# Cross-attention on one core: the next tile's transposes moved to the second half of a period's first block, and the first attention tile's low half moved from GpSimd to VectorE

## The reference, cut to what matters

```
def block_forward(x, codebook_embeds, codebook_mask, ...):
    xn = layer_norm(x, ln0_w, ln0_b)
    q, k, v = (heads of xn @ qkv_w.T)
    sa = merge(softmax(q @ k.T * SCALE) @ v) @ sa_proj_w.T
    x = x + sa
    xn = layer_norm(x, ln1_w, ln1_b)
    q = heads(xn @ q_w.T)
    k = heads(codebook_embeds @ k_w.T)
    v = heads(codebook_embeds @ v_w.T)
    attn = softmax(q @ k.T * SCALE + bias)
    x = x + merge(attn @ v) @ ca_proj_w.T
    xn = layer_norm(x, ln2_w, ln2_b)
    return x + (gelu(xn @ fc1_w.T + fc1_b) @ fc2_w.T + fc2_b)
```

## Time and profile before

| | |
|---|---|
| median of 3 runs | 3499.25 us (3497.89, 3499.25, 3512.89) |
| profiled execution | 3504.63 us, span 3502.8 us |
| PE busy, share of the span | 3281.3 us, 94% |
| DVE, ACT, POOL busy | 2078.2, 1541.9, 1553.9 us |
| mean granted clock of PE | 0.963 |
| cross phase in the trace | about 2058 to 2606 us |

### The profile page before, as it was taken

One profiled execution on the slowest core, in us unless ns is written; L12 is line 12 of the kernel. 1 busy time (PEld: TensorE's weight loads), 2 busy tenths in 40 slices (PEclk: granted clock), 3 DMA queues, 4 the chain that ended last, 5 costly groups with the idle time before them and its releaser, 6 DMA issues. The chain is left out here.

```text
span 3502.8 us, 44500 instructions
## 1 busy us (share of the span) xinstructions
PE 3281.3 (94%) x16812; PEld 2133.4 (61%) x16812; DVE 2078.2 (59%) x3643; ACT 1541.9 (44%) x2826; POOL 1553.9 (44%) x495
## 2 busy tenths in 40 slices
PE   7998999999999999999999959898969599999999
PEld 5885555555555555555555346656537488888887
DVE  4444887777778777777877136767657532222222
ACT  2321566666666666666666513443434321111111
POOL 0001578878887887888788723343401000000000
PEclk9997899999999999999999979999989899999999
DMA  4446265565557556555653554433337621111110
GB/s 169 179 169 182 56 149 117 113 155 129 121 126 152 123 109 150 124 125 126 151 119 83 106 150 137 125 113 119 101 125 274 242 103 41 41 45 48 41 44 25
DMA packets 195909, 420.93 MB, mean 120 GB/s; under 512 B 33601, under 2 KB 56711, under 8 KB 176239
## 3 DMA queue, kind: packets, MB, share of 16 engines
q1 hardware_dynamic: 172399, 281.75, 26.0%
q0 software_dynamic: 18432, 134.23, 19.0%
q10 hardware_dynamic: 4864, 2.11, 0.3%
HBM read 154.47 MB, written 102.82 MB: 73 GB/s over the span
## 5 line engine op out<-in xcount | busy, mean ns | idle before, releaser
L1787 DVE TENSOR_REDUCE self_part_max<-self_first 128x1 f32<-128x512 f32 x2048 | 1251.0, 680 | 345.9 <-PE self_first L1622 345.7
L1575 POOL TENSOR_TENSOR self_part_sum<-self_expo 128x2048 f32<-128x2048 f32 x256 | 1185.3, 4643 | 310.2 <-DMA self_part_sum<-self_part_sum 194.9
L1737 ACT ACTIVATE self_expo<-self_second 128x512 f32<-128x512 f32 x2048 | 1039.5, 625 | 481.9 <-PE self_second L1652 468.8
L1622 PE MATMUL self_first<-self_k,self_q 96*128 96x512 f32 x2048 | 855.0, 425 | 12.6 <-DMA self_k<-k_t 12.6
L1652 PE MATMUL self_second<-self_q,self_k 98*128 98x512 f32 x2048 | 827.9, 406 | 15.2 <-DVE self_max_low L1799 7.0
L1622 PEld LDWEIGHTS self_first<-self_k,self_q 96*128 96x128 f32 x2048 | 397.7, 194 | 301.0 <-DVE self_part_max L1787 163.0
L1665 PE MATMUL self_weighted<-self_expo,self_v_sb 128*32 128x512 f32 x4096 | 499.9, 606 | 0.0
L1652 PEld LDWEIGHTS self_second<-self_q,self_k 98*128 98x128 f32 x2048 | 386.5, 189 | 184.1 <-ACT self_expo L1737 52.6
L2127 DVE CAST mlp_h_high<-mlp_h 128x512 fp32r<-128x512 f32 x128 | 54.9, 429 | 507.1 <-PE mlp_out_sum L61 506.9
L2102 ACT ACTIVATE mlp_h<-mlp_hidden_sum,mlp_b_col 128x512 f32<-128x512 f32 x128 | 88.1, 688 | 603.5 <-PE mlp_hidden_sum L61 603.5
L1665 PEld LDWEIGHTS self_weighted<-self_expo,self_v_sb 128*32 128x32 f32 x4096 | 107.9, 110 | 233.3 <-ACT self_expo L1737 126.3
(11 more groups left out here) (176 smaller groups left out, 3879.8 us busy)
## 6 DMA issues: line engine op xcount, KB each, us to landing
self_part_sum<-self_part_sum POOLq DMA_DIRECT2D x128, 1024.0 KB, 9.0
self_k<-k_t SPq DMA_DIRECT2D x96, 256.0 KB, 11.2
self_q<-q_t SPq DMA_DIRECT2D x93, 256.0 KB, 4.9
cross_q<-cross_r_high SPq DMA_DIRECT2D x240, 64.0 KB, 2.0
qkv_x<-in_x SPq DMA_DIRECT2D x8, 1024.0 KB, 6.3
v<-qkv_v_sb SPq DMA_DIRECT2D x32, 256.0 KB, 2.1
q_t<-qkv_r_high SPq DMA_DIRECT2D x32, 256.0 KB, 2.0
q_t<-qkv_r_low SPq DMA_DIRECT2D x32, 256.0 KB, 2.3
```

The lines of the kernel that those rows point to most:

```text
L1575: nc.gpsimd.tensor_tensor(to, expo[:, t % p_slots], expo[:, (t + 1) % p_slots], ALU.add).then_inc(pair_done, 1)
L1622: nc.tensor.matmul(first[:, n % f_ring], q[0:base, c % q_slots, a, s * P:(s + 1) * P], k[0:base, c // stages_per_group % 2, a, k0:k0 + TOK ...
L1737: nc.scalar.activation(expo[:, t % p_slots, a], second[:, s_slot[n]], ACT.Exp, scale=scale).then_inc(exp_done, 1)
L1787: nc.vector.tensor_reduce(part_max[:, a * SUB + s, k:k + 1], first[:, n % f_ring], AX_X, ALU.max).then_inc(first_read, 1)
```

## The change

Two edits.

The first moves the four transposes of the next tile in a period's first block. Before, chunk c stands on PE behind pair n = 1, 3, 5 and 7. Now it stands behind n = 4, 5, 6 and 7. `high_turned` on ACT moves with it behind the exponentials of the same n, and `low_turned` on DVE from behind the maxima n = 2, 4, 6 and 7 to behind n = 5, 6, 7 and 7 (two in a row at the end). The last chunk keeps its place on every engine.

The second gives the subtraction `low_attn(0)` to DVE, ahead of the projection weights' low half. POOL's setting of `q` now waits for `w_ready` (DVE's weights' low half) instead of `a_ready`. The later tiles' `low_attn` stays on POOL.

```
@@ POOL @@
                 pool.wait_ge(rows_set, 1)
-                low_attn(0)
-                pool.wait_ge(a_ready, 1)
+                pool.wait_ge(w_ready, 1)
                 nc.gpsimd.memset(q[base:base + 4].bitcast(F32), 1.0).then_inc(rows_set, 1)
@@ PE, period(t) @@
                     for n in range(per_group):
                         second_pass(t, 0, n)
                         first_pass(t, 2, n)
-                        if n % 2 == 1 and has_next:
-                            turn(t + 1, n // 2)
+                        if n >= per_group - chunks and has_next:
+                            turn(t + 1, n - per_group + chunks)
@@ ACT, period(t) @@
-                        if n % 2 == 1 and has_next:
-                            high_turned(t + 1, n // 2)
+                        if n >= per_group - chunks and has_next:
+                            high_turned(t + 1, n - per_group + chunks)
@@ DVE, period(t) @@
                         maxima(t, 2, n)
-                        if n % 2 == 0 and n > 0 and has_next:
-                            low_turned(t + 1, n // 2 - 1)
+                        if n > items - chunks and has_next:
+                            low_turned(t + 1, n - items + chunks - 1)
@@ DVE, start of the phase @@
                 nc.vector.memset(ones[:], 1.0).then_inc(ones_done, 1)
+                dve.wait_ge(a_high_done, 1)
+                nc.vector.tensor_tensor(a_low[:], a_raw[:], a_high[:].bitcast(F32), ALU.subtract).then_inc(a_ready, 1)
                 dve.wait_ge(w_high_done, 1)
```

## The result

Twenty runs of each kernel: median 3507.57 us (3499.20 to 3515.75) against 3499.22 (3494.02 to 3512.89), a ratio of 1.0015 with an interval of 1.0008 to 1.0022. That is 2.8 to 7.7 us slower, 5.3 in the middle. The time lies in the range I gave and within the 0.5% that I called no change, but on the other side of my 1.5 us gain, and clear of noise.

The account below looks back on a forecast made before the run. PE was taken as the engine to watch, with two waits totalling 46 us as the most removable. First edit +0.8 and second -2.3 sum to -1.5 us, from the median 3499.25 to 3498 us, range 3488 to 3512.

Parts of the forecast that it names:

- The wait moves: First block: PE's wait for the norms moves from first transpose to third `first_pass`, ends 0.4 us later, 3.95 instead of 4.16.
- The block's price: First block of the six waiting periods: the new order costs 0.15 us in period 1, 0 to 0.15 in each other.
- my walk: PE's first block in period 1, stepped with its own strides, low clock ending at 2202.4 as before: +0.15 us.
- From that instruction on nothing differs: Period 1's first block: from `first_pass(t, 3, 2)`, at about 2206.0 instead of 2205.83, old and new order run alike.
- PE's own strides cover the slots: The other five waiting periods: where the clock comes back later, the two `dense` slots cost nothing extra; 0 to 0.15 us each.
- Period 0: First block without a wait for norms: the new order only bunches the transposes, losing 0.3 us.
- the clock comes back sooner: Rival, behind the first-block wait: low clock lasts 3.9 us instead of 5.6, 0.85 us saved a period, 3493; chance 8%.
- The start: Cross phase's start: with both subtractions on DVE, PE's first matmul comes at about 2073.5 instead of 2075.82, -2.3 us.
- Everything in the chain behind PE's start moves along: Tile 0's projection, norm and turning wait only for each other, so the start's 2.3 us carry through.
- the bound of 0: Start edit's worst case: no gain, if both subtractions take 4.97 us for another reason or the 3.9 us low clock grows equally.
- second falls: Rival: a second clock fall, 3.9 us as in period 2, comes in all six others, 23 us, 3521; chance 4%.
- stay up: Rival, first-block wait: the shorter idleness no longer pulls PE's clock down, 2.4 us in six periods, 14 us, 3484; chance 3%.

Follow-up runs that it names:

- norms_behind: Changed kernel, but from period 1 on the next tile's norms stand behind DVE's first-block maxima n = 1, 2, 3 and 3: 3495.06 us, ratio 0.9984.
- turns_only: The changed kernel without the second edit, so only the transposes are moved: 3507.46 us, ratio 1.0019.
- fillers: The changed kernel with 16 filler matmuls ahead of the third `first_pass` of periods 1 to 6: 3494.15 us, ratio 0.9977.
- norms_fill: Changed kernel with norms behind the first block's maxima and six filler matmuls ahead of the third `first_pass` of periods 1 to 6: 3493.17 us, ratio 0.9967.
- fillers_oldorder: The kernel before plus the second edit, with 17 filler matmuls ahead of the first transpose of periods 1 to 6: 3486.80 us, ratio 0.9953.
- block4_fillers: The changed kernel with two filler matmuls behind each of the first two pairs of every period's fourth block: 3504.98 us, ratio 1.0006.
- bias_filled: The changed kernel with the 12 fillers that stood behind the one-column bias matmuls spread among them: 3508.10 us, ratio 1.0014.

## Why the prediction was wrong

**The wait moves: right.** 3.93 us for 3.95 forecast, 0.4 us later, at the `first_pass` I named, and no gain from it. `norms_behind` shows its cause.

**The block's price: right in kind, too small.** I took 0.1 us for each of six periods, from 0.15 in period 1 and 0 to 0.15 in the others. It was 0.37 in the profile (0 in that of `turns_only`), and 0.54 at a steady clock. What failed is the lateness with which my walk let `first_pass(t, 3, 2)` come. Counted from the period's mark it stands 0.49 us later than before in period 1, and 0.29 to 0.37 later in the others. "From that instruction on nothing differs" held: the mark behind the second block is as late, by 0.48 and 0.29 to 0.37.

Two steps ahead of it were wrong. In period 1 I let the low clock end at its old instant, 10.9 us behind the mark; it ended 12.2 behind it, and the fourth transpose came 0.6 us late, not 0.3. For the other periods I wrote that "PE's own strides cover the slots". But in periods 2 to 6 the fourth transpose now stands 12.30 us behind the mark (11.87 to 12.16 before), each time directly behind the second chunk's low half, so the slot seems to set it. At the steady clock the third transpose has a printed wait for its slot (0.30 in the rows of `fillers`). I had also left out ACT: `second_pass(t, 1, 2)` now waits 0.17 to 0.22 us for an exponential and had no such wait before. The `first_pass` behind it waits longer still, for the maximum, as it did before.

**Period 0: wrong.** I took +0.3, by letting the low clock end at its old instant. The stretch lasted 3.4 us longer, because the order there was changed: +1.5 to 1.7 us. I had set down that case's opposite as a rival (the clock comes back sooner) and no rival for this side.

**The start: right at the first matmul, wrong at the next step.** "Everything in the chain behind PE's start moves along" failed: of 2.4 us nothing was left at the first `result` matmul in six of the twelve profiles of kernels with the edit and the bias matmuls in place (42.26 to 42.51 us; without the edit 41.89 to 42.13), and 2.2 to 2.9 were left in the other six (39.19 to 39.89). What was left did not show in the times either. I had named this case, the low clock growing by as much, as the bound of 0, and took nearly the whole.

**The sum.** Of my two terms, +0.8 and -2.3, the first was 3.7 us in the profile (1.5 for period 0 and 2.2 for periods 1 to 6) and 4.8 at a steady clock, and the second 0 to -1, not told from nothing in any time. Together they make 3 to 5 of the measured 2.8 to 7.7 us. The rest may be second falls, at 3 to 5 us each, but that is not shown. The six profiles with the moved transposes and no fillers have 1, 2, 2, 1, 2 and 2 of them, and the two with the old places 1 and 1. `fillers`, `norms_fill` and `fillers_oldorder` have 2 each, and the last has the old order, so that the order need not bring them. `block4_fillers` speaks for them as a part of the loss, but its interval does not settle it.

**The rivals.** The clock did not stay up by itself; with fillers it did, and gave 2.1 us a period where I had 2.4. The sooner clock, for which the Trainium skill's page "TensorE: Matmul & The Clock Gate" (section "PE-mode transpose") spoke, went the other way: where transposes stood early, in period 0, the clock came back sooner. The rule of the Trainium skill's page "SBUF — State Buffer" (section "Who interferes with whom") held, and the trace agrees: 2.29 and 2.28 us for the two subtractions with POOL idle, instead of 4.97 beside POOL's. The second fall did come, once or twice per execution, not in every period.

## What to carry to other kernels

Moving the consumer of a late result helps only if everything between is free of the same producer: here the third pair waited for VectorE, behind the very norms that the transposes had waited for. Walk a reordered block for each state of the clock, not for one period at the low clock: the two slots cost 0.54 us a period at the full clock, where the walk gave 0.1. And where a short gap or a stretch of narrow matmuls pulls PE's clock down, a few microseconds won just ahead of it may not arrive: fill the gap first (here 13 us and more, against the 5 that the reordering cost), and compare orders on top of that.

## What the runs showed of the hardware that I had not expected

- About period 0's beginning, with PE busy almost all along (13.36 of 13.64 us after, 10.09 of 10.24 before), the low stretch lasted 13.65 us when pairs of score matmuls came first (eight profiles), and 10.24 us with transposes between them (six).
- The clock can fall with PE busy without a gap: over the 32 bias matmuls of one column and the fillers behind them (9.53 us busy of 9.53, clock 0.64; and 8.06 of 8.06 in the stretch ahead, clock 1.00). With fillers among them, in `bias_filled`, it stayed up. In `turns_only` it fell at the `weigh` matmuls of period 4, but there PE had stood idle for 0.9 of the 9.3 us before.
- The low stretches behind the waits keep a distance of their own. In the changed kernel they begin at 2191.85, 2253.29, 2314.73, 2376.18, 2437.62 and 2499.05, 61.44 us apart to 0.01, while the periods last 61.45 to 61.86. That a period which runs a little faster would meet the clock's return at the same instant is my reading; no run tests it.
